# Two token tiles, three weight tiles and the last stage's preparation moved into the stages ahead of them

## Chip, cores and metric

The kernel is one program on one core of a Trainium2 chip. The metric is the device time of one execution in microseconds (us), as the median of several runs. TensorE (PE) multiplies, with its weight load shown apart as PEld; VectorE (DVE), ScalarE (ACT) and GpSimd (POOL) do elementwise work; SyncE (SP) issues the DMA transfers. Each engine executes its own instructions in order, and the engines wait for each other by semaphores.

## The reference, cut to what matters

The reference is a chain of four layers over 2048 tokens of width 512. Each layer adds its result to x. The parts that the change touches are these:

```
# layer 1, second half; layer 2, second half is alike, with a top-2 choice for the gates
base = x @ W_base.T + b_base
h    = einsum('nd,erd->ner', x, A);  moe = einsum('ner,ne,eor->no', h, weights, B) * 2
x    = x_old + base + moe
# layer 2, first half: attention with a paged cache
q, k, v = x @ Wq.T, x @ Wk.T, x @ Wv.T      # then norm, rotation, attention, and o @ Wo.T
# layer 3
y = einsum('bct,bcd->bdt', x, weights[subjects])      # a 32x32 mixing matrix per subject
x = x + y @ W.T + bias + sum over e of (coeffs*scales)[e] * (y @ A[e].T) @ Bf[e].T
```

## The kernel before

All arithmetic is float32, done as three matmuls on a high part and a low part of each operand (`mm3`, line 195). A high part is made by a copy on ACT, and the low part by a subtraction on DVE (`low_part`, line 200) or, for some weight tiles, on POOL. So a tile costs one ACT pass, then one DVE or POOL pass, before PE can use it.

The program is a sequence of stages, and each is a block in which every engine has its own program. At the end of a block all engines meet before any starts the next one. Memory that a stage takes for itself is free only inside it. The stages here are, in order:

- `moe(..., 1, Tables)`, the first mixture. It makes x2. It works on 16 tiles of 128 tokens, and stores each to HBM. Per tile, PE does the gates (12 matmuls of 138 columns into `pl`), one transposition of the weighted low-rank activations (`pt`, line 1628), the base product of the next tile (12 of 512 columns, into `po`) and the three matmuls that add the low-rank part to `po`. DVE computes the gates (lines 1531 to 1583), adds `po` to the old x in `xr` (line 1606, "the add"), makes the low part of `hT` and of a later input tile. `whole(tt + 1)` on PE waits until the add of tile tt-1 is done, since `po` has two banks. POOL adds the bias to each `xr` (line 1479) as soon as its old x has landed.
- `l2_qkv`, the projection. 8 groups of columns by 16 token tiles make 128 steps. Each has 24 matmuls, 12 of 512 and 12 of 256 columns. At its head SP fetches three weight tiles (`w.fetch`, line 134), waits for the last stores of x2, fetches two token tiles, then the fourth weight tile into the slot that the first one leaves. PE transposes two token tiles (line 1942), ACT and DVE split weights and tokens, and PE starts step 0 when all four weight tiles and the first token tile are split.
- `l2_attn`, the attention, and `l2_out`, the output projection. The latter is 4 column blocks by 32 steps of 12 matmuls of 512 columns. POOL has nothing to do in the last half of it.
- `moe(..., 2, Blocks)`, the second mixture. It is as the first, with a top-2 gate. `Blocks` is the work that rides along: it builds the block-diagonal mixing matrices `bd` of layer 3, by 16 masks (line 1378), 4 copies on ACT and 4 low parts on DVE during tiles 2 to 5.
- `l3`, the last stage. It first loads `araw`, `braw` and `whole`, scales `braw`, splits both, multiplies them (24 matmuls into `pm`), adds the product to `whole` and splits that as `base` (called the fold below). Then, per tile, 12 matmuls of 128 columns mix the tokens (`mixed`, into `pc`), ACT and DVE split the result as `cT`, and 12 of 512 columns give `po`. DVE adds it to x, and SP stores.

## Time and profile before

| what | value |
|---|---|
| median of 3 runs | 3490.33 us (3486.12 to 3491.93) |
| the profiled execution, its own time | 3486.69 us |
| its span, first to last instruction | 3484.9 us |
| mean granted clock of TensorE | 0.976 |
| PE busy in the span | 3303.1 us (95%) |
| DVE, ACT, POOL busy | 2325.4, 1764.9, 1369.3 us |

The profiled execution takes 1.8 us more than its span. Since PE is busy nearly everywhere, what matters are the few places where it waits or runs at the lower clock. The two mixtures, the head of the projection and the head of the last stage hold several of them.

### The profile page before, as it was taken

The page shows a single profiled execution, that of the slowest core. Times are in us where ns is not written, and L with a number is a line of the kernel's source. Part 1 is how long each engine was busy: PE and PEld are TensorE (multiplying, and loading weights), DVE is VectorE, ACT ScalarE, POOL GpSimd, SP SyncE. Part 2 cuts the span into 40 slices and gives each one's busy share as a digit, 9 for nine tenths or more (in the row PEclk, how much of TensorE's full clock was granted, in tenths as well). Part 3 has the DMA queues.
Part 4 walks back from the last instruction along what each step waited for, and adds up shares of the span by engine and source line. Part 5 has one row for each costly group of instructions (what it writes and reads, how often), then busy time and mean ns, then how long its engine had stood idle before and what let it go on. Part 6 is the DMA issues. An engine that isn't in the chain of part 4 may idle for free. (4 is left out here: it accounts for less than half of the span.)

```text
span 3484.9 us, 69495 instructions
## 1 busy us (share of the span) xinstructions
PE 3303.1 (95%) x22214; PEld 3048.6 (87%) x22214; DVE 2325.4 (67%) x6609; ACT 1764.9 (51%) x4303; POOL 1369.3 (39%) x2426
## 2 busy tenths in 40 slices
PE   7799799999989999999799999989999998999988
PEld 5688699988878888888799999989999998888877
DVE  6444444445457777778888888888888886322274
ACT  4322222233227778788566666656666665322212
POOL 0221100000017878888556555555555552100022
PEclk9899899999999999999899999999999999999999
DMA  5410532234545555556766666656666666533333
GB/s 204 131 59 26 135 95 81 74 113 130 187 160 162 181 168 179 183 173 206 230 215 218 210 216 216 208 181 207 214 215 213 211 216 195 177 109 109 109 124 124
DMA packets 456501, 571.95 MB, mean 164 GB/s; under 512 B 171657, under 2 KB 341449, under 8 KB 439242
## 3 DMA queue, kind: packets, MB, share of 16 engines
q1 hardware_dynamic: 436426, 429.08, 39.5%
q0 software_dynamic: 19712, 138.42, 11.3%
q8 instruction: 180, 2.95, 0.4%
q14 instruction: 183, 1.50, 0.1%
HBM read 394.60 MB, written 172.75 MB: 163 GB/s over the span
## 5 line engine op out<-in xcount | busy, mean ns | idle before, releaser
L2316 PE MATMUL l2a_x<-l2a_pt,l2a_V 128*128 128x128 f32 x4096 | 542.5, 275 | 4.4 <-DVE l2a_pn L2257 3.6
L2316 PEld LDWEIGHTS l2a_x<-l2a_pt,l2a_V 128*128 128x128 f32 x4096 | 503.2, 193 | 5.0 <-issue 4.9
L2234 DVE CUSTOM_DVE_ANT_0 l2a_sm<-l2a_s,l2a_B 128x544 f32<-128x544 f32 x512 | 369.6, 722 | 92.6 <-PE l2a_s L195 80.4
L1479 POOL TENSOR_TENSOR moe_xr<-moe_xr,moe_bias 128x512 f32<-128x512 f32 x32 | 42.1, 1318 | 960.7 <-DMA moe_xr<-s_x 960.6
L2184 ACT ACTIVATE l2a_p<-l2a_sm,l2a_st 128x544 f32<-128x544 f32 x512 | 379.8, 742 | 27.9 <-DVE l2a_st L2237 27.6
L2043 POOL CAST l2a_K<-cache 128x256 fp32r x768 | 294.4, 433 | 223.4 <-issue 223.4
L2043 POOL CAST keys<-cache 128x256 fp32r x750 | 298.4, 447 | 188.2 <-issue 112.0
L2170 ACT ACTIVATE l2a_pt<-l2a_t 128x512 f32<-128x512 f32 x512 | 305.6, 597 | 128.3 <-PE l2a_t L2302 128.0
L2302 PE MATMUL l2a_t<-ident,l2a_p 128*128 128x128 f32 x2048 | 336.1, 287 | 5.4 <-ACT l2a_ao L2177 5.4
L2302 PEld LDWEIGHTS l2a_t<-ident,l2a_p 128*128 128x128 f32 x2048 | 288.4, 210 | 6.5 <-issue 5.9
L2248 DVE TENSOR_SCALAR l2a_p<-l2a_p,l2a_st 128x512 f32<-128x512 f32 x512 | 280.8, 548 | 18.2
L2177 ACT ACTIVATE l2a_ao<-l2a_x 128x128 f32<-128x128 f32 x512 | 142.0, 277 | 280.8 <-PE l2a_x L2317 280.8
L195 PE MATMUL l2a_s<-keys,head 128*128 128x288 f32 (+1 forms) x1536 | 261.7, 306 | 18.8 <-POOL l2a_K L2043 8.7
L195 PE MATMUL l2q_pa<-keys,cache 128*128 128x512 f32 (+1 forms) x1024 | 268.5, 344 | 0.0
L195 PE MATMUL l2q_pa<-l2q_w1H,cache 128*128 128x512 f32 (+1 forms) x1024 | 267.7, 344 | 0.0
L195 PE MATMUL l2a_s<-l2a_K,l2a_Q 128*128 128x288 f32 (+1 forms) x1536 | 259.9, 305 | 3.4 <-POOL l2a_K L2043 3.0
L1802 POOL TENSOR_TENSOR l2q_rot<-l2q_qs,sinq 128x256 f32<-128x256 f32 x256 | 197.7, 792 | 130.3 <-ACT l2q_qs L1851 130.3
L195 PEld LDWEIGHTS l2a_s<-keys,head 128*128 128x128 f32 x1536 | 214.4, 192 | 19.9 <-issue 13.4
L195 PEld LDWEIGHTS l2a_s<-l2a_K,l2a_Q 128*128 128x128 f32 x1536 | 213.6, 191 | 3.8 <-issue 3.3
L1824 ACT ACTIVATE l2q_qn<-l2q_qn,l2q_r 128x128 f32<-128x128 f32 x640 | 200.3, 397 | 0.8 <-DVE l2q_qn L1917 0.8
L195 PEld LDWEIGHTS l2q_pa<-keys,cache 128*128 128x128 f32 x1024 | 181.0, 190 | 21.7
L195 PEld LDWEIGHTS l2q_pa<-l2q_w1H,cache 128*128 128x128 f32 x1024 | 180.2, 189 | 21.6
(766 smaller groups left out, 8715.1 us busy)
## 6 DMA issues: line engine op xcount, KB each, us to landing
s_qT<-l2q_qo SPq DMA_DIRECT2D x128, 512.0 KB, 2.9
head<-s_qT SPq DMA_DIRECT2D x64, 512.0 KB, 5.8
l2a_Q<-s_qT SPq DMA_DIRECT2D x64, 512.0 KB
s_ao<-l2a_ao SPq DMA_DIRECT2D x64, 512.0 KB, 4.9
l2o_a<-s_ao SPq DMA_DIRECT2D x128, 256.0 KB, 3.0
s_kn<-l2q_ko SPq DMA_DIRECT2D x128, 128.0 KB, 3.1
head<-s_kn SPq DMA_DIRECT2D x32, 512.0 KB, 6.0
l2q_stage<-in_wqkv SPq DMA_DIRECT2D x32, 384.0 KB, 4.1
```

The source lines that it names most:

```text
L195: i = pe.matmul(out, a, b, start=start and m + z == 0, stop=stop and 3 * m + z == n - 1)
L1479: pool.tensor_tensor(xr[tt][:, :], xr[tt][:, :], bias[:, :], ALU.add).then_inc(biased, 1)
L1802: pool.tensor_tensor(r[:, hs, a], q[:, hs, z], sn[:, y, tt, :].unsqueeze(1).broadcast_to([P, hs.stop - hs.start, 64]), ALU.mult).then_inc( ...
L1824: act.activation(o[:, h, :], o[:, h, :], ACT.Copy, scale=f[:, 10 + h:11 + h]).then_inc(scaled, 1)
L2043: e.tensor_copy(K[:, j:j + 1, :, :].rearrange("p a z n -> p a (z n)"), Kall[:, bass.ds(v, 1), :, :].rearrange("p a z n -> p a (z n)")).the ...
L2170: act.activation(ptr[tr % 2][:, :, :], ps_t[tr % 2][:, :, :], ACT.Copy).then_inc(t_copied, 1)
L2177: act.activation(ao[k][:, hg, :, 32 * (g % 2):32 * (g % 2) + 32], ps_x[pv % 2][:, P:256].rearrange("p (h s) -> p h s", h=4), ACT.Copy).the ...
L2184: act.activation(prr[sc % 6][:, :], smr[sc % 2][:, :], ACT.Exp, bias=s[:, 1:2], scale=SCALE, accum_out=s[:, 2:3]).then_inc(exped, 1)
L2234: dve.tensor_tensor_reduce(out=smr[sc % 2][:, :], in0=ps_s[sc % 2][:, 224:768], in1=Br[g % 2][:, :], scale=1.0, scalar=-3e38, op0=ALU.add, ...
L2248: dve.tensor_scalar(p[:, 0:512], p[:, 0:512], s[:, 3:4], None, ALU.mult).then_inc(scaled, 1)
L2302: m = pe.transpose(ps_t[tr % 2][:, k, :], p[:, k:512:4], ident[:, :])
L2316: pe.matmul(px[:, P:256], V[:, k * D + hg * P:k * D + hg * P + P], pt[:, k, :], start=k == 0, stop=False)
```

## The change

In both mixtures the bias is added on DVE (`with_bias`), one tile ahead, and POOL has no work there. Each mixture calls the work that rides along on SP, ACT, DVE and PE.

In the first mixture `Tables` also fetches the first three weight tiles of the projection (tiles 4 to 6) and loads, transposes and splits the first two tiles of x2 (SP in tiles 8 and 9, PE in 11 and 12, ACT in 12 and 13, DVE in 13 and 14). The projection finds them ready. It fetches only the fourth weight tile and begins step 0 with a part for each of the first three weight tiles, as they are split. DVE makes all four low parts there.

`Blocks` moves from the second mixture to the output projection (column block 2). `Fold`, the last stage's preparation, moves into the second mixture. It also loads and splits the first three token tiles of x3. `l3` starts with `mixed(0)`.

The core of the diff:

```diff
     def by_pool(self, k):
-        return self.pooled and k % 3 == 2
+        return self.pooled and k % 3 == 2 and k >= self.own
...
+    def late(self, sp, tt, stores):
+        if 4 <= tt < 7:
+            k = tt - 4
+            sp.dma_start(self.w[k][:, :].unsqueeze(1), rows_of(self.A["wqkv"][0], k, 1)).then_inc(self.w_in[k], 16)
+        if 8 <= tt < 10:
+            t = tt - 8
+            sp.wait_ge(*stores.landed(t, 2))
+            sp.dma_start(self.nat[t][:, :], self.x[t * P:(t + 1) * P, :]).then_inc(self.nat.sem(t), 16)
+
+    def on_vector(self, dve, tt, banks):
+        if 13 <= tt < 15:
+            t = tt - 13
+            dve.wait_ge(self.hi, t + 1)
+            low_part(dve, self.xT[t], banks[t][:, :].rearrange("p (k n) -> p k n", k=4)).then_inc(self.lo, 1)
+
+    def on_scalar(self, act, tt, banks):
+        if 12 <= tt < 14:
+            t = tt - 12
+            act.wait_ge(self.turned, t + 1)
+            act.activation(self.xT[t][0], banks[t][:, :].rearrange("p (k n) -> p k n", k=4), ACT.Copy).then_inc(self.hi, 1)
...
+    def on_tensor(self, pe, tt, banks, weighed):
+
+        if 11 <= tt < 13:
+            t = tt - 11
+            pe.wait_ge(*self.nat.landed(t))
+            pe.wait_ge(weighed, 13 + t)
+            for k in range(4):
+                i = pe.transpose(banks[t][:, k * P:(k + 1) * P], self.nat[t][:, k * P:(k + 1) * P], self.ident[:, :])
+            i.then_inc(self.turned, 1)
...
+    def mask(self, dve, m):
...
+        for j in range(4):
+            dve.tensor_scalar(self.wx(m)[:, :, j, :], self.wg[:, 4 * m:4 * m + 4, :], self.jm[:, j:j + 1], None,
+                              ALU.mult).then_inc(self.masked, 1)
+
+    def high(self, act, m):
+        act.wait_ge(self.masked, 4 * m + 4)
+        act.activation(self.bd[0][:, 4 * m:4 * m + 4, :, :], self.wx(m), ACT.Copy).then_inc(self.hi, 1)
+
+    def low(self, dve, m):
+        dve.wait_ge(self.hi, m + 1)
+        low_part(dve, sl(self.bd, S_, slice(4 * m, 4 * m + 4), S_, S_), self.wx(m)).then_inc(self.lo, 1)
+
+
...
+    def late(self, sp, tt, stores):
+        if tt == 1:
+            sp.dma_start(self.whole[:, :, :], rows_of(self.A["base3"], 0, 4)).then_inc(self.whole_in, 16)
+        if 6 <= tt < 9:
+            t = tt - 6
+            sp.wait_ge(*stores.landed(t, 2))
+            sp.dma_start(self.xn[t][:, :], self.src[t * P:(t + 1) * P, :]).then_inc(self.xn.sem(t), 16)
+
+    def on_scalar(self, act, tt, banks):
+        if tt == 2:
+            act.wait_ge(self.a_in, 16)
+            act.activation(self.a3[0][:, :, :], self.araw[:, :, :], ACT.Copy).then_inc(self.a_hi, 1)
...
+        if tt == 4:
+            act.wait_ge(self.b_scaled, 2)
+            act.activation(self.b3[0][:, :, :], self.braw[:, :, :], ACT.Copy).then_inc(self.b_hi, 1)
+        if 8 <= tt < 11:
+            t = tt - 8
+            act.wait_ge(*self.xn.landed(t, 1))
+            act.activation(self.xh[t][0][:, :], self.xn[t][:, :], ACT.Copy).then_inc(self.x_hi, 1)
+        if tt >= 12:
+            k = tt - 12
+            act.wait_ge(self.folded, k + 1)
+            act.activation(self.base[0][:, k, :], self.whole[:, k, :], ACT.Copy).then_inc(self.base_hi, 1)
+
+    def on_vector(self, dve, tt, banks):
...
+        if tt == 4:
+            dve.wait_ge(self.a_hi, 1)
+            low_part(dve, sl(self.a3, S_, S_, S_), self.araw[:, :, :]).then_inc(self.a_lo, 1)
+        if tt == 6:
+            dve.wait_ge(self.b_hi, 1)
+            low_part(dve, sl(self.b3, S_, S_, S_), self.braw[:, :, :]).then_inc(self.b_lo, 1)
+        if 9 <= tt < 12:
+            t = tt - 9
+            dve.wait_ge(self.x_hi, t + 1)
+            low_part(dve, sl(self.xh[t], S_, S_), self.xn[t][:, :]).then_inc(self.x_lo, 1)
+        if 12 <= tt < 16:
+            k = tt - 12
+            if k == 0:
+                dve.wait_ge(self.whole_in, 16)
+            dve.wait_ge(self.fold_mm, k + 1)
+            dve.tensor_tensor(self.whole[:, k, :], self.whole[:, k, :], banks[k][:, :], ALU.add).then_inc(self.folded, 1)
+        if tt >= 13:
+            k = tt - 13
+            dve.wait_ge(self.base_hi, k + 1)
+            low_part(dve, sl(self.base, S_, k, S_), self.whole[:, k, :]).then_inc(self.base_lo, 1)
+
+    def on_tensor(self, pe, tt, banks, weighed):
+
+        k = tt - 11
+        if 0 <= k < 4:
+            if k == 0:
+                pe.wait_ge(self.a_lo, 1)
+                pe.wait_ge(self.b_lo, 1)
+            pe.wait_ge(weighed, 13 + k)
+            mm3(pe, banks[k][:, :], [(sl(self.a3, S_, m, slice(k * P, (k + 1) * P)), sl(self.b3, S_, m, S_))
+                                     for m in range(2)]).then_inc(self.fold_mm, 1)
...
-        @block.gpsimd
-        def _(pool):
-            pool.wait_ge(bias_in, 16)
-            for tt in range(NT):
-                pool.wait_ge(*xr.landed(tt, 1))
-                pool.tensor_tensor(xr[tt][:, :], xr[tt][:, :], bias[:, :], ALU.add).then_inc(biased, 1)
...
+            def with_bias(tt):
+                if tt < NT:
+                    dve.wait_ge(*xr.landed(tt, 1))
+                    dve.tensor_tensor(xr[tt][:, :], xr[tt][:, :], bias[:, :], ALU.add).then_inc(biased, 1)
...
                 parts(tt + 4)
-                if tt > 1:
-                    next(side, None)
-                    next(side, None)
+                with_bias(tt + 1)
+                beside.on_vector(dve, tt, pl)
...
                 lora(tt + 1)
+                beside.on_tensor(pe, tt, pl, weighed)
...
-    w = Weights(st, 3, 768, [(*sl(wq[hg % 2], S_, slice(k, k + 1), S_), rows_of(A["wqkv"][hg], k, 1)) for hg in range(8) for k in range(4)])
...
+    w = Weights(st, 3, None, [(*sl(wq[hg % 2], S_, slice(k, k + 1), S_), rows_of(A["wqkv"][hg], k, 1)) for hg in range(8) for k in range(4)],
+                own=4, bufs=S["wq_raw"], sems=S["wq_in"])
...
-            for k in range(3):
-                w.fetch(sp, k)
-            sp.dma_start(tab[:, :], A["table"].rearrange("(a n) -> a n", a=1)[:, 0:16]).then_inc(tab_in, 16)
+            w.fetch(sp, 3)
             for k in range(10, 16):
                 sp.wait_ge(*before_x.landed(k))
-            x_tile(0)
-            x_tile(1)
-            w.fetch(sp, 3)
             x_tile(2)
             x_tile(3)
+            sp.dma_start(tab[:, :], A["table"].rearrange("(a n) -> a n", a=1)[:, 0:16]).then_inc(tab_in, 16)
...
             for k in range(4):
-                if not w.by_pool(k):
-                    w.low(dve, k)
-            tokens(0)
-            tokens(1)
+                w.low(dve, k)
...
+            def part(n, ks, cols):
+
+                hg, tt = steps[n]
+                return mm3(pe, pa[n % 2][:, cols], [(sl(xT[tt], S_, k, S_), sl(wq[hg % 2], S_, k, cols)) for k in ks],
+                           start=ks[0] == 0, stop=ks[-1] == 3)
+
+            columns = (slice(0, 512), slice(512, 768))
+            for k in range(3):
+                w.ready(pe, k)
+                for cols in columns:
+                    part(0, (k,), cols)
             for n, (hg, tt) in enumerate(steps):
                 if hg == 0:
                     tokens(tt + 2)
-                    pe.wait_ge(x_lo, tt + 1)
+                    if tt >= 2:
+                        pe.wait_ge(x_lo, tt - 1)
                 if tt == 0:
                     w.ready_to(pe, 4 * hg + 3)
                 if n >= 2:
                     pe.wait_ge(v_copied, n - 1)
-                for cols in (slice(0, 512), slice(512, 768)):
-                    i = mm3(pe, pa[n % 2][:, cols], [(sl(xT[tt], S_, k, S_), sl(wq[hg % 2], S_, k, cols)) for k in range(4)])
+                for cols in columns:
+                    i = part(n, range(4) if n else (3,), cols)
...
     parts = [st.pair(f"as{i}", [P, D]) for i in range(4)]
     acc = [[st.ps(f"acc{j}{i}", [P, D]) for i in range(4)] for j in range(2)]
...
                 if k == 31:
                     for m in range(4):
                         i = 4 * cb + m
                         act.wait_ge(out_mm, n + 1)
...
+                if cb == 2 and k % 4 == 0 and k < 16:
+                    blocks.mask(dve, k // 4)
+                if cb == 2 and k % 4 == 3 and k < 16:
+                    blocks.low(dve, k // 4)
...
-                if tt < NT:
+                if NF <= tt < NT:
...
-            sp.dma_start(cf[:, :], A["coef"]).then_inc(cf_in, 16)
-            sp.dma_start(sc[:, :], A["scal"]).then_inc(sc_in, 16)
-            sp.dma_start(braw[:, :, :], rows_of(A["bt3"], 0, 2)).then_inc(braw_in, 16)
-            sp.dma_start(araw[:, :, :], rows_of(A["a3n"], 0, 2)).then_inc(a3_in, 16)
-            tokens(0)
-            tokens(1)
-            sp.dma_start(whole[:, :, :], rows_of(A["base3"], 0, 4)).then_inc(base_in, 16)
+            tokens(3)
             sp.dma_start(bias[:, :], row_bc(A["b3"], D)).then_inc(bias_in, 16)
-            for tt in range(2, 6):
+            for tt in range(4, 6):
...
-            pe.wait_ge(a_lo, 1)
-            pe.wait_ge(b_lo, 1)
-            for k in range(4):
-                if k >= 2:
-                    pe.wait_ge(folded, k - 1)
-                mm3(pe, pm[k % 2][:, :], [(sl(a3, S_, m, slice(k * P, (k + 1) * P)), sl(b3, S_, m, S_)) for m in range(2)]).then_inc(fold_mm, 1)
-            pe.wait_ge(bd_made, 4)
             mixed(0)
             mixed(1)
...
                     pe.wait_ge(added, tt - 2)
                 pe.wait_ge(c_lo, tt + 1)
-                if tt == 0:
-                    pe.wait_ge(base_lo, 4)
                 mm3(pe, po[tt % 3][:, :], [(sl(cT[tt % 3], S_, k, S_), sl(base, S_, k, S_)) for k in range(4)]).then_inc(out_mm, 1)
                 mixed(tt + 2)
```

Where instructions stand is shown at three places. In such rows and in those of the trace, `moe` names either mixture where buffer numbers are left out. The first is DVE in the first mixture, in the middle of the loop, around the add of tile 3 (`xr3`). Before:

```order
L1583 TENSOR_TENSOR moe1_hw5<-moe1_pl1,moe1_sm1 128x128
L1606 TENSOR_TENSOR moe1_xr3<-moe1_xr3,moe1_po1 128x512
L200 TENSOR_TENSOR moe1_hT0L<-moe1_pt0,moe1_hT0H 128x128
L200 TENSOR_TENSOR cache<-moe1_dr4,cache 128x512
L1531 TENSOR_REDUCE moe1_sm2<-moe1_pl2 128x1
L1533 RECIPROCAL moe1_sm2<-moe1_sm2 128x1
```

After, the same place:

```order
L1708 TENSOR_TENSOR moe1_hw5<-moe1_pl1,moe1_sm1 128x128
L1737 TENSOR_TENSOR moe1_xr3<-moe1_xr3,moe1_po1 128x512
L200 TENSOR_TENSOR moe1_hT0L<-moe1_pt0,moe1_hT0H 128x128
L200 TENSOR_TENSOR cache<-moe1_dr4,cache 128x512
L1719 TENSOR_TENSOR moe1_xr4<-moe1_xr4,moe1_bias 128x512
L1656 TENSOR_REDUCE moe1_sm2<-moe1_pl2 128x1
L1658 RECIPROCAL moe1_sm2<-moe1_sm2 128x1
```

Between the low part of the input tile and the gates of the next tile there is one more pass of 128x512, the bias for tile 4.

The second place is SP from the last stores of the first mixture into the projection (`l2q_stage` and `wqraw` are raw weight tiles, `l2q_nat` raw token tiles). Before:

```order
L1470 DMA s_x<-moe_xr 128x512 x5
L1435 UNCONDITIONAL_BRANCH
L1713 UNCONDITIONAL_BRANCH
L134 DMA l2q_stage<-in_wqkv 128x768 x3
L1747 DMA l2q_tab<-in_table 1x16
L1719 DMA l2q_nat<-s_x 128x512 x2
L134 DMA l2q_stage<-in_wqkv 128x768
L1719 DMA l2q_nat<-s_x 128x512 x3
```

After:

```order
L1601 DMA s_x<-moe_xr 128x512 x5
L1566 UNCONDITIONAL_BRANCH
L1846 UNCONDITIONAL_BRANCH
L134 DMA wqraw<-in_wqkv 128x768
L1852 DMA l2q_nat<-s_x 128x512 x2
L1883 DMA l2q_tab<-in_table 1x16
L1852 DMA l2q_nat<-s_x 128x512
```

Three weight fetches and two token fetches have gone from the head, and the fetch of the fourth weight tile comes first, ahead of the token tiles 2 and 3.

The third place is DVE from the end of the second mixture into the last stage (`moe_` is the mixture, `l_` the last stage). Before:

```order
L1606 TENSOR_TENSOR moe_xr<-moe_xr,moe_po 128x512
L1435 UNCONDITIONAL_BRANCH
L2551 UNCONDITIONAL_BRANCH
L2565 TENSOR_TENSOR l_cw<-l_cf,l_sc 128x2
L2569 TENSOR_SCALAR l_braw<-l_braw,l_cw 128x512 x2
L200 TENSOR_TENSOR l_a3L<-l_araw,l_a3H 128x1024
L200 TENSOR_TENSOR l_b3L<-l_braw,l_b3H 128x1024
L200 TENSOR_TENSOR l_xh0L<-l_xn,l_xh0H 128x512
L200 TENSOR_TENSOR l_xh1L<-l_xn,l_xh1H 128x512
L2579 TENSOR_TENSOR l_whole<-l_whole,l_pm 128x512 x4
L200 TENSOR_TENSOR l_baseL<-l_whole,l_baseH 128x512 x4
```

After:

```order
L200 TENSOR_TENSOR moe_hT3L<-moe_pt,moe_hT3H 128x128
L1719 TENSOR_TENSOR moe_xr<-moe_xr,moe_bias 128x512
L1505 TENSOR_TENSOR moe_whole<-moe_whole,moe_pl 128x512
L200 TENSOR_TENSOR base3L<-moe_whole,base3H 128x512
L1737 TENSOR_TENSOR moe_xr<-moe_xr,moe_po 128x512
L1505 TENSOR_TENSOR moe_whole<-moe_whole,moe_pl 128x512
L200 TENSOR_TENSOR base3L<-moe_whole,base3H 128x512 x2
L1566 UNCONDITIONAL_BRANCH
L2662 UNCONDITIONAL_BRANCH
L200 TENSOR_TENSOR l_cT0L<-l_pc,l_cT0H 128x512
```

The fold's passes now stand in the mixture's last tiles, three of them behind the last add, and the first thing that DVE does in the last stage is the low part of the first mixed tile.

## Rows read from the trace of the kernel before

**Rows 1.** Busy time by stretch: projection, output projection; PE, PEld, DVE, ACT, POOL, clock, DMA

```profile
core 0: us, PE busy (x) PEld busy (x) DVE busy (x) ACT busy (x) POOL busy (x), PEclk, DMA share, GB/s
1126.00:1196.00 70.00, 70.00 (x427) 62.38 (x426) 55.30 (x105) 56.35 (x154) 58.29 (x77) 1.00 0.56 178
3110.00:3200.00 90.00, 90.00 (x398) 74.51 (x398) 22.84 (x33) 23.04 (x38) 0.00 (x0) 1.00 0.35 109
```

**Rows 2.** Timeline, head of the projection: start, duration, engine, instruction, [idle before]

```profile
1028.58 1.31 SPq L134 DMA_DIRECT2D l2q_stage<-in_wqkv  x3
1033.72 0.33 SPq L134 DMA_DIRECT2D l2q_stage<-in_wqkv  x1
1035.16 1.97 PE L1942 MATMUL l2q_pt<-ident,l2q_nat 128*128 128x128 f32 x8 [8.06 <-DMA l2q_nat<-s_x]
1037.22 0.84 ACT L138 ACTIVATE keys<-l2q_stage 128x768 fp32r<-128x768 f32 x1 [1.89 <-DMA l2q_stage<-in_wqkv]
1038.10 0.96 DVE L143 TENSOR_TENSOR head<-l2q_stage,keys 128x768 fp32r<-128x768 f32 x1 [3.44 <-ACT keys L138]
1046.62 0.70 ACT L1851 ACTIVATE l2q_qs<-l2q_pa 128x640 f32<-128x640 f32 x1 [5.09 <-PE l2q_pa L195]
```

**Rows 3.** Waits of PE in the first mixture (936 to 1028): total, times, longest

```profile
PE moe_po L195 <- DVE moe_xr L1606: 2.3, 3, 1.1
PE moe_po L195 <- DVE cache L143: 1.7, 1, 1.7
```

**Rows 4.** The same in the second mixture (3300 to 3396)

```profile
PE moe_po L195 <- DVE moe_xr L1606: 7.9, 6, 2.0
PE moe_po L195 <- DVE moe_hT3L L200: 0.9, 1, 0.9
```

**Rows 5.** Timeline, second mixture: one DVE instruction twice, and POOL beside the second

```profile
3320.93 0.17 DVE L1566 CUSTOM_DVE_ANT_0 moe_sm<-moe_sm 128x8 f32<-128x8 f32 x1
3346.47 1.27 DVE L1566 CUSTOM_DVE_ANT_0 moe_sm<-moe_sm 128x8 f32<-128x8 f32 x1
3346.45 1.28 POOL L1479 TENSOR_TENSOR moe_xr<-moe_xr,moe_bias 128x512 f32<-128x512 f32 x1 [5.08 <-DMA moe_xr<-s_x]
```

**Rows 6.** Timeline of both mixtures: transpositions, the DVE passes behind them, PE behind an add

```profile
986.16 0.29 PE L1628 MATMUL moe_pt<-ident,moe_hw 128*128 128x128 f32 x1
986.80 0.29 DVE L200 TENSOR_TENSOR moe_hT3L<-moe_pt,moe_hT3H 128x128 fp32r<-128x128 f32 x1 [0.88 <-ACT moe_hT3H L1507]
990.13 0.68 DVE L1606 TENSOR_TENSOR moe_xr<-moe_xr,moe_po 128x512 f32<-128x512 f32 x1
991.09 0.29 PE L1628 MATMUL moe_pt<-ident,moe_hw 128*128 128x128 f32 x1
3360.44 0.29 DVE L200 TENSOR_TENSOR moe_hT0L<-moe_pt,moe_hT0H 128x128 fp32r<-128x128 f32 x1 [1.05 <-ACT moe_hT0H L1507]
3363.64 0.69 DVE L1606 TENSOR_TENSOR moe_xr<-moe_xr,moe_po 128x512 f32<-128x512 f32 x1 [0.15 <-PE moe_po L195]
3318.26 0.68 DVE L1606 TENSOR_TENSOR moe_xr<-moe_xr,moe_po 128x512 f32<-128x512 f32 x1
3318.99 0.51 PE L195 MATMUL moe_po<-moe_baseH,ahead 128*128 128x512 f32 x1 [1.66 <-DVE moe_xr L1606]
```

**Rows 7.** Timeline, last stage: four DVE passes of 128x512 with both inputs in SBUF

```profile
3413.98 2.49 DVE L200 TENSOR_TENSOR l_baseL<-l_whole,l_baseH 128x512 fp32r<-128x512 f32 x4
```

**Rows 8.** Chain that ended last, in order of time, head of the last stage

```profile
3396.11 0.33 SPq L2493
...
3397.46 4.99 DMA l_araw<-in_a3n
...
3406.07 7.28 PE l_pm L195 x24
...
3417.72 3.07 PE l_po L195 x12
3420.80 1.29 PE l_pc L195 x12
```

**Rows 9.** Timeline: PE entering the second mixture, and SP's last stores in it

```profile
3300.39 7.92 PE L195 MATMUL moe_pl<-ahead 128*128 128x136 f32 x36 [2.96 <-PEq L2347]
3379.21 16.48 SPq L1470 DMA_DIRECT2D s_x<-moe_xr  x5
```

193 lines of the change are left out of this document (89 added, 104 removed).

## Prediction

> **What bounds the kernel now.** I read the busy time by stretch first. In the long projection PE is busy in all of the 70 us of a stretch, DVE in 55.3, ACT in 56.4 and POOL in 58.3; in the output projection PE is busy in 90 of 90 us, and DVE and ACT in 22.8 and 23.0 [rows 1]. So PE sets the time there, and a gain can only come from where PE waits or runs at half rate. The waits and timelines show four such places: the head of the projection [rows 2], the loops of the two mixtures [rows 3, 4], and the head of the last stage, where the chain that ended last leaves PE for a load, for ACT and for DVE [rows 8]. The change touches exactly these four. I take them in turn, against the profiled execution's own time of 3486.69 us.
>
> **Bias on DVE, both mixtures.** Two things move. First, DVE no longer shares its time with a busy POOL. The same instruction takes 0.17 us alone and 1.27 us where it starts 0.02 us behind a POOL bias of 1.28 us; it ends when POOL does [rows 5]. The Trainium skill (SBUF — State Buffer, "Who interferes with whom") says that a DVE instruction that uses the port shared with GpSimd is held for the whole of the other's instruction, and counts among these any DVE instruction with two SBUF inputs. By that rule 32 holds of up to 1.28 us would vanish, up to 41 us of DVE time; the trace says that only PE's waits for DVE can be won. These are 2.3 and 1.7 us in the first mixture and 7.9 and 0.9 in the second [rows 3, 4].
>
> Second, DVE pays 16 biases in each mixture. Four passes of this size with both inputs in SBUF take 2.49 us, so 0.6 us one [rows 7]. Does it show? Between a transposition and PE's use of the add that depends on it lie: 0.64 us to the next DVE pass, 3.33 us from there to the add, and 0.73 us from the add's start to PE: 4.70 us in the first mixture. In the second the middle piece is 3.20 less the 0.15 that DVE waited, so 3.05, and the chain is 4.42 [rows 6]. PE itself goes from one transposition to the next in 4.93 us [rows 6], so both chains are hidden. With 0.6 more they are 5.30 and 5.02: late by 0.37 and 0.09. A late PE makes its next transposition late too, so every second round has slack, and half of it counts: 0.18 and 0.05 us a round. Over 12 rounds that is 2.2 us and 0.5 us. What could be dearer: at POOL's price, 1.28 us a bias [rows 5], 0.34 us more a round, 4 us more in each mixture. At nothing, the 2.7 us are gained instead. I take 0.6, since rows 7 are of the same engine, size and memory.
>
> **First mixture.** Of its waits of 2.3 us the last, about 0.7 us, ends with PE's own last matmuls and stays, so 1.6 and 1.7 go. The bias costs 2.2. Eight transpositions are added; 12 matmuls of 128 columns take 1.29 us [rows 8], so these take 0.9, of which 0.4 fall into the lateness above. ACT and DVE passes for the two token tiles come when DVE has no more input tiles to split. The five loads on SP have many rounds ahead of them. Sum: 3.3 - 2.2 - 0.5 = 0.6 us gained.
>
> **Head of the projection.** Before, from SP's first issue (1028.58) to ACT's first copy of a result (1046.62) pass 18.0 us [rows 2]. After, call the stage's start B. ACT splits the first weight tile at once (0.84), DVE makes its low part (0.96 [rows 2]), so at B+2.0 both SP may fetch the fourth tile and PE may start. The fetch took 3.5 us before (1033.72 to 1037.22), then 0.84 and 0.96 follow [rows 2]: B+7.4. PE meanwhile does 18 matmuls at half rate. In the last stage 24 matmuls of 512 columns that began cold took 7.28 us, and 12 warm ones take 2.86 [rows 8]; 7.28 - 5.72 = 1.6 us is what a cold start costs once. Warm, a quarter of a step (3 of 512, 3 of 256 columns) is 1.1 us. Three of them and the loss are 4.9, so PE is at B+6.9, transposes a token tile (0.5), and finishes the last quarter at B+8.5. Gain: 18.0 - 8.5 = 9.5 us. It hangs on the fourth tile: the loads that SP issued at 1028.58 in a bunch made ACT wait longer, and with 2 us more for this load the gain is 7.5. If PE stays at half rate throughout, 1 us goes.
>
> **Masks in the output projection.** Four times DVE gets about 0.9 us of masks and, three steps on, 0.7 us of low part; a step there is 2.7 us, of which DVE uses a quarter [rows 1]. PE hides it. Without that cover it would be 6 us. Cost: 0.
>
> **Second mixture.** All waits for adds but none of the work go: 7.9 + 0.9 = 8.8 us, the last 1.5 of them filled by folding matmuls. Added are 24 folding matmuls, 5.7 at the warm pace [rows 8]; the bias, 0.5; two low parts of 128x1024 on DVE (tiles 4 and 6), twice the size of rows 7, 1.2 us each against a chain without slack, so 2.3; and three low parts of x3 tiles, 0.6 each at half weight, 0.9. SP's new loads are issued behind those that the loop needs. Sum: 8.8 - 5.7 - 0.5 - 2.3 - 0.9 = -0.6.
>
> **Head of the last stage.** Before, SP ends its last store issue at 3379.21 + 16.48 = 3395.69 [rows 9], the stage begins at 3396.11, and PE's first real output matmul starts at 3417.72 [rows 8]: 22.0 us. After: behind the last add stand an addition to `whole` and two low parts, the second behind an ACT pass, 2.0 us; the last add itself comes 0.5 later, since DVE is still busy with a piece of the fold. SP issues its last store (0.33, as an issue in [rows 8]) beside this, and entering the stage takes 0.42 (3395.69 to 3396.11). So PE begins to mix 2.0 + 0.5 - 0.33 + 0.42, about 2.5 us, after the point from which the 22.0 were counted. PE has then idled 3 us, as it had at 3300.39, where 36 short matmuls took 7.92 us, 0.22 each, against 0.11 warm [rows 8, 9]. So 24 mixing matmuls take 5.3 us, which covers ACT and DVE on the first mixed tile, and the first output block loses 1.6 us to the clock as `pm` did. That is 2.5 + 5.3 + 1.6 = 9.4 against 22.0: 12.6 us gained. Warm from the start it would be 3 us less, bounded by ACT and DVE on the first tile; with 3 us more at half rate, 1.5 more.
>
> **Sum.** 0.6 + 9.5 + 0 - 0.6 + 12.6 = 22.1 us. The profiled execution would take 3464.6 us; the median of the runs, 3490.33, lies 3.6 above the profiled one, so it becomes 3468.2. I say 3468.
>
> **Rivals.**
> - *The clock rises within the mixing* (the last stage gains 3 us more), or the chains in the mixtures have more slack than I give them (2.7 more): about 3463. For it: `pm` was warm after some 3 us. Against: 36 short matmuls stayed at half rate [rows 9]. 0.2.
> - *DVE becomes the bound of both mixtures.* A round then loses 0.5 us and not 0.18, because a pass waits for its old x or costs more than 0.6; 8 to 10 us go back: 3477. DVE is the engine that PE waits for already [rows 4]. 0.1.
> - *The change doesn't do what it says at the projection*: the fourth weight tile and the stores of x2 set its start as before, 5 us of 9.5 are not won: 3473. For it: the fetch still stands behind DVE's first low part. Against: it has no token tiles ahead of it. 0.1.
> - *Slower.* The projection is 128 steps in a fixed rhythm, where POOL has only 12 of 70 us idle [rows 1]. If the new phase between DVE and POOL at its head makes them hold each other [rows 5] so that PE waits in each step, it costs 128 times the wait. From 0.17 us a step on it eats the whole gain; at 0.25 us the time is 3500. Against: 70 of 70 us busy, over many phases of the weight work. 0.03.
>
> **How the numbers follow.** The forecast itself has 0.55, the rivals 0.2, 0.1, 0.1, 0.03, and 0.02 is for anything else. The median of before spans 5.8 us over three runs, and 0.2% is 7 us, about what a measurement can tell. The forecast's own range is 3465 to 3472. To leave out no more than 2 in 10, 3459 to 3477 takes in the first three rivals and the bounds of bias and load. Faster 0.95, within 0.2% 0.02, slower 0.03.
>
> **What would show it.** Right: no waits of PE for `xr` over 0.6 us in the mixtures, but many small ones; ACT's first copy in the projection some 8.5 us after SP's first issue; `l_pc` matmuls 0.22 us apart at the head of the last stage and the first `l_po` 8 us behind the last store issue; no new wait in the output projection. Wrong: waits on `moe_xr` loads by DVE, a fourth weight tile that lands later than 5.5 us into the projection, or PE waits between its steps.

## The result

The changed kernel takes **3457.87 us** (median of 4 runs, 3452.21 to 3460.31) against 3490.82 for the kernel before on the same chip (4 runs, 3486.12 to 3491.93). The ratio is 0.9906, 95% interval [0.9889, 0.9923], so 27 to 39 us of gain. I forecast 3468 and 22 us, with 3459 as the lower end: the sign and the places were right, the size was 11 us short, and the measured time lies 1.1 us under the range. The profiled execution took 3457.95 us, its span is 3456.2.

The page of the changed kernel gives span and busy time:

```profile
span 3456.2 us, 69511 instructions
PE 3306.9 (96%) x22214; PEld 3052.9 (88%) x22214; DVE 2328.6 (67%) x6640; ACT 1766.3 (51%) x4305; POOL 1325.0 (38%) x2393
```

Busy time by stretch, the same two as in [rows 1] (the columns are those named there):

```profile
1126.00:1196.00 70.00, 70.00 (x428) 62.38 (x427) 55.42 (x105) 56.28 (x153) 58.42 (x77) 1.00 0.53 169
3110.00:3200.00 90.00, 90.00 (x398) 74.52 (x398) 27.61 (x52) 26.75 (x45) 0.00 (x0) 1.00 0.35 110
```

PE is still busy in all of both. The masks are now visible in the second, as 4.8 us more of DVE and 3.7 of ACT than in [rows 1], and PE does not feel them.

Timeline of the changed kernel at the head of the projection, beside [rows 2]:

```profile
1023.07 2.31 ACT L138 ACTIVATE keys<-wqraw 128x768 fp32r<-128x768 f32 x3 [3.07 <-PEq L1566]
...
1024.93 0.33 SPq L134 DMA_DIRECT2D wqraw<-in_wqkv  x1
1024.96 0.80 PE L195 MATMUL l2q_pa<-keys,cache 128*128 128x512 f32 x1 [3.44 <-DVE head L143]
...
1028.13 0.84 ACT L138 ACTIVATE keys<-wqraw 128x768 fp32r<-128x768 f32 x1 [2.75 <-DMA wqraw<-in_wqkv]
...
1029.01 0.96 DVE L143 TENSOR_TENSOR head<-wqraw,keys 128x768 fp32r<-128x768 f32 x1 [2.37 <-ACT keys L138]
...
1032.25 0.71 ACT L1977 ACTIVATE l2q_qs<-l2q_pa 128x640 f32<-128x640 f32 x1 [0.44 <-PE l2q_pa L195]
```

From ACT's first pass to its first copy of a result pass 9.2 us; I had said 8.5. The fourth weight tile landed after 3.2 us and not 3.5.

Waits of PE in the changed kernel, for the first mixture (to 1023) and then the second, beside [rows 3, 4]:

```profile
PE moe_po L195 <- DVE moe_hT3L L200: 0.9, 1, 0.9
PE moe_po L195 <- DVE moe_xr L1737: 0.7, 1, 0.7
...
PE moe_pl L195 <- PEq L2481: 3.0, 1, 3.0
PE moe_po L195 <- DVE moe_xr L1737: 2.1, 3, 0.9
PE moe_po L195 <- DVE moe_btL L143: 0.4, 1, 0.4
```

What is left for `moe_xr` in the second mixture are 2.1 us, where there were 7.9.

The chain that ended last, head of the last stage, beside [rows 8]:

```profile
3382.14 5.35 PE l_pc L195 x24
3387.49 5.04 PE l_po L195 x12
3392.53 1.29 PE l_pc L195 x12
3393.82 2.83 PE l_po L195 x12
```

It now begins with PE itself. The 24 mixing matmuls run at half rate as forecast (5.35 us, granted clock 0.50), and so does nearly the whole first `l_po`: 5.04 against 2.83 in the next, 2.2 us lost where I had 1.6.

### Where the gain sits

I cut each profile at the same events: PE's first gate matmul of a mixture, PE's last matmul in it, ACT's first copy in the projection. Before was profiled five times in all and the changed kernel three times (the added ones are experiments below). Means and ranges, in us:

| stretch | before | changed | gain | forecast |
|---|---|---|---|---|
| start to first mixture (code unchanged) | 935.8 (932.4 to 937.4) | 933.3 (932.5 to 934.2) | 2.5 | 0 |
| first mixture | 91.1 (89.7 to 92.7) | 88.4 (88.2 to 88.6) | 2.7 | 0.6 |
| its end to ACT's first copy in the projection | 19.5 (18.5 to 19.9) | 10.6 (10.5 to 10.7) | 8.9 | 9.5 |
| from there to the second mixture | 2255.1 (2253.8 to 2257.1) | 2254.3 (2252.1 to 2255.4) | 0.9 | 0 |
| second mixture | 94.9 (92.5 to 96.1) | 91.7 (91.2 to 92.2) | 3.2 | -0.6 |
| its end to the end of the kernel | 91.9 (90.3 to 93.5) | 76.8 (75.9 to 77.5) | 15.1 | 12.6 |
| sum | 3488.3 | 3455.0 | 33.3 | 22.1 |

The trace on which the forecast was built has 937.4, 89.7, 19.5, 2253.8, 94.2 and 90.3 in these rows. The first mixture and the last stage stand there at or next to the lower end of what the kernel before does, and the code ahead of the first mixture next to the upper end.

### The profile page after: what moved, and what is told of

It is laid out like the page before. It is cut to its first block and busy times, and to the rows that moved or that the text cites. A ratio compares the mean times of both kernels' runs of the same rounds, so it can differ in the third digit from the quotient of the medians.

```text
span 3456.2 us, 69511 instructions
## 1 busy us (share of the span) xinstructions
PE 3306.9 (96%) x22214; PEld 3052.9 (88%) x22214; DVE 2328.6 (67%) x6640; ACT 1766.3 (51%) x4305; POOL 1325.0 (38%) x2393
## 5 line engine op out<-in xcount | busy, mean ns | idle before, releaser
L2367 DVE CUSTOM_DVE_ANT_0 l2a_sm<-l2a_s,l2a_B 128x544 f32<-128x544 f32 x512 | 369.9, 722 | 94.2 <-PE l2a_s L195 81.8
L195 PEld LDWEIGHTS l2a_s<-keys,head 128*128 128x128 f32 x1536 | 214.7, 192 | 18.5 <-issue 11.8
```

The costliest lines, as they stand in the source:

```text
L195: i = pe.matmul(out, a, b, start=start and m + z == 0, stop=stop and 3 * m + z == n - 1)
L2367: dve.tensor_tensor_reduce(out=smr[sc % 2][:, :], in0=ps_s[sc % 2][:, 224:768], in1=Br[g % 2][:, :], scale=1.0, scalar=-3e38, op0=ALU.add, ...
```

## The experiments

The surplus is the 11 us by which the gain is larger than forecast. Theory at first: the terms of the forecast are right within their bounds, and the surplus is chance or one mis-sized term. Rivals: it belongs to one part that does more than I said, or the parts do not add. A hold, below, is a DVE instruction that takes longer because a POOL instruction runs beside it.

### Parts undone, one at a time

**The bias alone.** Everything but the bias as before:

```diff
-            for tt in range(NT):          # POOL
-                pool.tensor_tensor(xr[tt][:, :], xr[tt][:, :], bias[:, :], ALU.add).then_inc(biased, 1)
+                with_bias(tt + 1)         # DVE, behind parts(tt + 4)
```

> Of the change only the bias on DVE, in both mixtures; projection, masks and last stage as before. Terms on record: first mixture 3.3 - 2.2 = 1.1 us gained, second 8.8 - 0.5 = 8.3 us, together 9.4: about 3481.4 from a median of 3490.8. PE waits for DVE of about 1 us in the middle of a round of the first mixture, none over 0.6 in the second. Rival 'DVE gets full': the biases cost what the holds did, 3488 to 3491. Rival 'the surplus sits here': the part of the 33 us that no term explains (about 8 to 10) comes from the bias, 3472 or less.

Measured: 3483.64 against 3488.42, ratio 0.9987 [0.9979, 0.9996]: 1 to 7 us gained. That is less than 9.4. The first mixture took 88.0, the second 93.1: 3.1 and 1.8 us under the means of before, where the terms had 1.1 and 8.3. Of the waits for adds in the second mixture that [rows 4] show as 7.9 us, this is left, without POOL:

```profile
PE moe_po L195 <- DVE moe_xr L1631: 4.5, 3, 1.9
```

So most of them were not POOL's doing.

**The bias on POOL, all else changed** (the reverse edit in the changed kernel).

> The changed kernel with the bias back on POOL, all else as changed. If the terms add, 9.4 us are given back: about 3467 from 3457.9. If DVE is so full of the fold's passes that its holds by POOL cost more now, 3470 or more. If the bias gave nothing once the second mixture carries the fold, 3458 to 3460.

Measured: 3465.52, ratio 0.9930 [0.9917, 0.9942]. Against the changed kernel's 0.9906 to 0.9912 that gives 6 to 8 us back. First mixture 92.9, second 97.7: 4.5 and 6.0 over the changed kernel, more than the bias won alone (3.1 and 1.8). By one profile of each the parts do not add. The medians do not settle it, since 6 to 8 us back and 1 to 7 us won overlap, and 7.6 lies near the 9.4 of the terms. With DVE's bias the side work is nearly free in the first mixture (88.0 without it, 88.4 with it).

**The projection's part undone**: loads, transpositions and the order of the projection's head as before.

> The changed kernel with the projection and the first mixture's side work as before (no early fetch, no early transposes; bias on DVE stays). Terms on record: head 9.5, side work -0.5: 9 us given back, 3467. The trace of the changed kernel shows 8.8 us at the head. Rival 'the surplus sits in the projection's new start': over 12 us given back, 3470 or more, with the difference between the head and the second mixture.

Measured: 3470.67, ratio 0.9949 [0.9936, 0.9963]. The head took 20.5 where the changed kernel has 10.5 to 10.7 and the kernel before 18.5 to 19.9. The profiled span stands 10.4 to 16.5 us above those of the changed kernel, the median 13 us above its median. That median is what the rival asked for (3470 or more). In the profile only 9.9 of the 12.9 us over the mean of the changed kernel are at the head, and the other 3 are spread over all other stretches but the first mixture. So the head gives 9 to 10 us, and a surplus there is not shown.

**The last stage's part undone**: masks beside the second mixture, fold in the last stage.

> The changed kernel with masks in the second mixture and the last stage's preparation in the last stage, as before; bias on DVE stays. Terms on record: 12.6 us given back at the head of the last stage, 8.9 us of side work taken off the second mixture: 3457.9 + 3.7 = 3461.6. Rival 'the fold is hidden in the second mixture' (its 24 matmuls fill waits that stay without them): up to 12.6 given back, 3470. Rival 'fold costs more than thought' : 3458 or less.

Measured: 3474.86, ratio 0.9963 [0.9950, 0.9976], 17 us over the changed kernel where I expected 3.7. End of the second mixture to the end of the kernel: 90.7, 14 us more. But the second mixture, rid of the fold, was not 9 us shorter; it took 93.2, longer than with the fold, because the masks were back in it. The expectation had left them out.

**Nothing beside the second mixture**: masks in the output projection, fold in the last stage.

```diff
-            st = moe(nc, A, S, st, 2, Fold)
+            st = moe(nc, A, S, st, 2, Nothing)   # and l3 does the fold itself, as before
```

> The changed kernel with nothing beside the second mixture: masks stay in the output projection, but the last stage's preparation is done in the last stage as before. Head of the last stage 23 us again, +14.5. Terms on record: the second mixture loses 8.9 us of fold, so 3459 + 12.6 - 8.9 = 3463. Rival 'the 24 matmuls are all that the fold costs' (two 128x1024 low parts and three x3 low parts hidden): second mixture 91.2 - 5.7 = 85.5, 3468. Rival 'the fold fills waits': second mixture 88 or more, 3471 or more.

Measured: 3467.34, ratio 0.9932 [0.9918, 0.9945]; second mixture 86.7. These are the waits of PE in the second mixture, first with masks only (the run before), then with nothing:

```profile
PE moe_po L195 <- DVE moe_xr L1656: 6.1, 5, 1.9
...
PE moe_po L195 <- DVE moe_hT3L L200: 0.9, 1, 0.9
```

```profile
PE moe_po L195 <- DVE moe_hT3L L200: 0.9, 1, 0.9
PE moe_po L195 <- DVE moe_xr L1664: 0.7, 1, 0.7
```

So the masks cost 6.5 us there even without POOL: in four rounds DVE gets two more pieces, 0.9 and 0.7 us. The fold costs 5.0: 6.6 in the rounds and behind them, less 1.7 at the entry, where the changed kernel came from its first gate to the second transposition in 15.7 to 16.6 us and this run in 17.8. I had booked the fold's 24 matmuls, its two long low parts and its x3 tiles as 8.9 of new cost.

The second mixture in steps, as means where there are several profiles: 94.9 before, 93.1 to 93.5 with the bias on DVE (three profiles), 86.7 with the masks gone too, 91.7 with the fold in it. My forecast took all of PE's waits for adds there as POOL's doing; the masks had most of them.

### What makes the kernel before scatter

**Changed kernel and kernel before, profiled again.**

> The changed kernel as it is, profiled again. The four changed places should repeat within 1 us: first mixture 88.4, head of the projection 10.7, second mixture 91.2, head of the last stage 8.6. If the 4.3 us by which the unchanged work ahead of the first mixture was shorter is chance, that piece comes out anywhere from 932 to 937 and the median lies at 3488.4 - 26 to 28 = 3460 to 3462. Rival 'it is an effect of the change': 933.1 again and a median of 3456 to 3458.

> The kernel before, profiled again. Two things are open: whether the 937.4 us ahead of the first mixture (931.9 to 935.5 in eight profiles of kernels with the same code there) were chance, and where the 3.6 to 5.5 us sit by which the medians of before lie above its profiled execution. If chance: 932 to 936 ahead of the first mixture, and the mixtures, heads and the rest longer than 89.7, 19.5, 94.2, 23.1 by some us. If it is an effect of how the kernel before lies in memory: 937 again, and the same in every stage.

> The kernel before a third time, one look: the same question as for its second profile.

> The changed kernel a third time. Mixtures 88.5 and 91.4 within 0.3 again, since no engine shares DVE's time; the stages ahead of the first mixture anywhere in 931 to 937 if their scatter is chance.

Measured: changed 3460.57 and 3457.25, ratios 0.9912 [0.9897, 0.9928] and 0.9909 [0.9894, 0.9924]; before against itself 1.0006 [0.9996, 1.0016], with the second profile at 3493.47 and the third at 3494.63 us. The waits in the second profile of before, first and second mixture:

```profile
PE moe_po L195 <- DVE moe_xr L1606: 4.2, 5, 1.2
...
PE moe_po L195 <- DVE cache L143: 1.3, 1, 1.3
...
PE moe_po L195 <- DVE moe_xr L1606: 5.5, 4, 2.0
```

In the third:

```profile
PE moe_po L195 <- DVE moe_xr L1606: 4.7, 7, 1.2
...
PE moe_po L195 <- DVE moe_xr L1606: 8.7, 6, 2.6
```

No two are alike, nor like [rows 3, 4]. The time from one transposition of PE to the next (a round; start to start, worked out from the timelines) shows it, for the first mixture, second to eighth interval:

| kernel | rounds, us |
|---|---|
| before, first profile | 5.02, 4.87, 5.69, 4.88, 4.87, 4.88, 4.93 |
| before, second | 6.05, 4.87, 5.48, 6.31, 4.88, 4.88, 4.92 |
| before, third | 6.10, 4.87, 5.46, 6.30, 4.88, 5.90, 4.92 |
| before, fourth | 5.86, 4.86, 4.87, 5.87, 4.88, 4.88, 4.92 |
| before, fifth | 4.93, 4.87, 5.84, 4.87, 4.88, 5.07, 4.92 |
| changed, first | 4.93, 5.23, 4.93, 5.21, 4.95, 5.21, 4.99 |
| changed, second | 4.92, 5.23, 4.90, 5.26, 4.89, 5.27, 4.93 |
| changed, third | 4.92, 5.23, 4.90, 5.25, 4.91, 5.24, 4.96 |

The changed kernel repeats itself within 0.07 us here. In the second mixture its first round varies (5.6, 5.9 and 6.5) and the others repeat as well. When POOL starts, a load decides: of 615.5 us of POOL's idle time before its 16 additions, 615.4 end with the landing of an old x (second profile, first mixture). The timeline of the same profile shows POOL and DVE meeting in the second mixture:

```profile
3331.32 0.87 DVE L1378 TENSOR_SCALAR moe_wx<-wg,moe_jm 128x128 f32<-128x128 f32 x4
...
3332.89 0.69 DVE L200 TENSOR_TENSOR bdL<-moe_wx,bdH 128x512 fp32r<-128x512 f32 x1 [0.70 <-ACT bdH L1389]
...
3333.59 1.28 POOL L1479 TENSOR_TENSOR moe_xr<-moe_xr,moe_bias 128x512 f32<-128x512 f32 x1 [3.69 <-DMA moe_xr<-s_x]
...
3334.04 0.86 DVE L1556 CAST moe_sm<-moe_ix 128x2 f32<-128x2 uint32 x1
...
3337.07 0.50 PE L195 MATMUL moe_po<-moe_baseH,moe_dT5H 128*128 128x512 f32 x1 [2.04 <-DVE moe_xr L1606]
...
3340.44 0.17 DVE L1556 CAST moe_sm<-moe_ix 128x2 f32<-128x2 uint32 x1
```

The same cast of 128x2 elements takes 0.17 us alone and 0.86 beside POOL, and ends 0.03 us after POOL does. It is in a chain of small steps that ends in `moe_xr`. The wait of 2.04 us is not all its work, for the same round carries a mask step and its low part (0.87 and 0.69).

Over whole mixtures the two causes part. I compared each DVE instruction of a mixture with the shortest of its kind there (same line, tiles and shape). In each of the 15 mixtures in which POOL works (two in each of seven profiles, one in the kernel that moves only the second bias), 7 to 12 DVE instructions take over 0.12 us longer, in sum 4.8 to 9.8 us, and every one of them overlaps a POOL instruction. In the 25 mixtures without POOL not a single one does. So POOL lengthens DVE's work in every execution, at other places each time.

**Is it the hold, or the wait for POOL's result?** One run without any bias, and one in which POOL works at the same points on data that nobody uses:

```diff
+                pool.tensor_tensor(junk[:, :], bias[:, :], bias[:, :], ALU.add).then_inc(biased, 1)
...
-                dve.wait_ge(biased, tt + 1)
+                dve.wait_ge(*xr.landed(tt, 1))
```

> Leaves out the addition of the bias in both mixtures (32 DVE instructions of the changed kernel), all else as changed. By the terms on record the biases cost 2.2 us in the first mixture and 0.5 in the second once POOL no longer holds DVE: 2.7 us faster, first mixture 86.2, second 90.7. Rival 'hidden': both as they were. Rival 'DVE is the bound': 0.68 us a round for 12 rounds in each, 12 us or more faster in all.

> As the run without a bias, but POOL does an addition of the same size at the same points on tiles that nobody else reads or writes (bias + bias into a spare tile), so nobody waits for POOL. The output lacks the bias. If POOL's work holds DVE's (the theory on record): mixtures near those with the bias on POOL, 92.9 and 97.7 less at most 1 us each, and 10 us over the run without bias: 3463. Rival 'the gain came from no longer waiting for POOL's result': 87 and 90 as without a bias, 3453.

Measured: without bias 3453.34, ratio 0.9892 [0.9877, 0.9907]; with POOL beside it 3458.44, ratio 0.9911 [0.9894, 0.9927]. First to last transposition: 72.5 and 77.2 us in the two mixtures without, 75.2 and 80.2 with POOL. POOL's instructions were shorter here, 1.04 against 1.28 us. So its mere presence costs 2.6 and 3.0 us in this pair of profiles, nobody waiting for it (1.8 and 4.6 over the whole mixtures): the hold is real, though smaller than the 10 us expected. With POOL doing the true bias the two stretches were 79.0 and 84.9. That is no proof of a wait for POOL's result, for there the holds were longer too: 8.3 and 8.8 us in sum against 5.3 and 4.8. The two are not parted. The Trainium skill (SBUF — State Buffer, "Who interferes with whom") names the cast among the instructions that can take the ports shared by DVE and GpSimd, when their operands meet certain conditions, and says that the first to issue keeps them for its whole instruction; the 0.86 us cast agrees.

The run without bias also prices DVE's: 74.5 - 72.5 = 2.0 us in the first mixture (2.2 forecast) and 2.0 in the second (0.5 forecast). In the second it falls where DVE has side work: the rounds with the fold's long low parts take 5.46 and 5.45 us without the bias and 6.03 and 6.05 with it, the one with the last x3 tile 4.89 and 5.49.

**Two more looks at before, and a kernel between.**

> Before, one look. Chance: 931 to 936 ahead of the first mixture. Effect of the change: 936 to 938. Mixtures 89.5 to 93 and 94 to 97 in either case, scattered.

> Before, one more look, with the same expectation: 931 to 936 ahead of the first mixture if the difference is chance, 936 to 938 if it is an effect; mixtures scattered.

> Of the change only the bias of the second mixture on DVE; POOL keeps the bias of the first. If POOL's work is what makes a mixture scatter: second mixture as with the bias alone (93.1 to 93.2, the same round times within 0.1), first between 89.7 and 92.5 with late rounds at other places than in any run before. Time between before and the bias alone: 3486 to 3489.

Measured: 3490.65 and 3488.32 us; ahead of the first mixture 935.8 and **932.4**. The last value lies within those of the runs made from the changed kernel, with the same code there (930.6 to 935.5), so the 2.5 us in the unchanged code are no effect that these runs can establish. The kernel with only the second bias moved: 3487.43, ratio 0.9992 [0.9983, 1.0001]; first mixture 92.4 with rounds of 8.97, 6.16 and 6.45, second 93.5. Its four long rounds, 7.07, 6.33, 6.32 and 6.37, are those of the run with only the last stage undone (7.08, 6.28, 6.33, 6.37). The run with the bias alone had the same mixture code and two rounds of 8.6 instead, so without POOL there are two patterns, not one.

### Single prices in the changed kernel

**The two low parts of 128x1024, halved:**

```diff
-        if tt == 4:
-            low_part(dve, sl(self.a3, S_, S_, S_), self.araw[:, :, :]).then_inc(self.a_lo, 1)
+        if 4 <= tt < 6:
+            low_part(dve, sl(self.a3, S_, tt - 4, S_), self.araw[:, tt - 4, :]).then_inc(self.a_lo, 1)
...                                                    # b3 likewise in tiles 6 and 7
```

> The changed kernel with the two low parts of 128x1024 (the fold's a3 and b3) cut into four of 128x512, one in each of tiles 4 to 7. If each long pass makes one round late by 1.1 us (6.02 and 6.05 against 4.9): two such rounds go, four of 5.2 to 5.5 come, 1 us gained in the second mixture, the rest as in the changed kernel. If lateness is not linear but a matter of slack: nothing is late but by 0.2, 2 us gained. Rival: the wait moves to the fold matmuls, no change.

Measured: 3458.65, ratio 0.9916 [0.9902, 0.9929], no difference in the median. In the profile the rounds of 6.02 and 6.05 became 5.49 and 5.50, with no other round longer by more than 0.2: 1 us, as the first theory said, and too little for the run times to tell.

**Matmuls that nobody reads, where PE only waits for a stage to end:**

```diff
+            idle_matmuls(pe, pt[0][:, :], hT[3][0][:, :], bt[0][:, 0, :], 6 if kind == 1 else 12)  # end of moe
+            idle_matmuls(pe, pa[1][:, 0:512], xT[0][0][:, 0, :], xT[0][0][:, :, :], 7)             # head of l2_qkv
+            idle_matmuls(pe, acc[0][0][:, :], wo[0][:, 31, 0:P], parts[3][0][:, :], 11)            # end of l2_out
```

> The changed kernel with matmuls whose result nobody reads, put where PE has nothing to do but wait for a stage to end: 11 behind the output projection, 6 behind the first mixture and 7 at the head of the projection, 12 behind the second mixture, each 512 columns. If idle time is what takes the clock down: first gates of the second mixture 36 in 4 us and not 5.8 to 7.9 (2 to 4 gained), 24 l_pc in 2.7 and not 5.2 and the first l_po 12 in 2.8 and not 5.0 (4.7 gained), 1 to 2 us in the projection's head: 7 to 9 us under the changed kernel, 3450. Rival: the clock falls anyway over the stage's boundary, or matmuls of zero use hold the stage's end: no change or up to 2 us slower.

> The run with unread matmuls at stage ends, and 15 more of them around the last block of the stage ahead of the first mixture (7 while PE waits for DVE's td, 8 behind its last matmul). There 24 matmuls of 256 columns ran 0.21 us apart against 0.12, and the 36 first gates took 4.7 to 6.9 against 4.2 warm: 2 us and 1 to 2 us to be gained. 3449 against 3452.6. Rival: what follows waits for DVE and the weights anyway, 3452 or more.

> Halved low parts, and unread matmuls behind the first mixture (6), at the head of the projection (7) and behind the second mixture (12), none behind the output projection. The head of the projection 1 us and the last stage 4.5 to 5 us shorter, second mixture 1 to 2: 6 to 8 us under the changed kernel. If the matmuls behind the output projection were of use, it is slower than the run that had them.

Measured: 3452.64, 3456.89 and 3451.72, ratios 0.9893 [0.9878, 0.9908], 0.9898 [0.9882, 0.9915] and 0.9894 [0.9881, 0.9908]; the changed kernel beside them 0.9912, none on that chip, and 0.9909. The first has all the lines above. The second has 15 more unread matmuls ahead of the first mixture and was no faster for them, as its rival had it (3452 or more). The third has the halved low parts and leaves out those behind the output projection. The profiles split it by place. Chain of the first of the three, head of the last stage:

```profile
3380.93 1.54 PE l_pc L195 x12
...
3382.49 0.60 ACT l_cT0H L2664
```

Twelve mixing matmuls in 1.54 us, not at half rate, and now the chain goes over ACT, because PE is no longer the slower. From the end of the second mixture's own matmuls to the end of the kernel pass 73.0 us in all three, against 75.9 to 77.5 in the changed kernel and 75.5 to 77.4 in other runs with its last stage, so 2.5 to 4.5 us are won. At the projection's head no gain is shown: 9.9, 10.2 and 9.9 us, and 9.9 to 10.7 in runs without unread matmuls. At the head of the second mixture nothing is won:

```profile
3285.22 4.21 PE L195 MATMUL moe_pl<-ahead 128*128 128x136 f32 x36 [0.47 <-PEq L2489]
3290.56 0.79 PE L195 MATMUL moe_po<-moe_baseH,ahead 128*128 128x512 f32 x1 [1.13 <-DVE moe_baseL L143]
```

That is the first of these kernels. The gates took 4.21 us (granted clock 1.00) instead of 7.92 in the third, which has no unread matmuls there, and PE then waited for the weights' low parts, with the clock down again (0.50 from 3290.60 to 3293.00). From the first gate to the second transposition it took 16.7 us with them and 16.6 without. At the head of the first mixture, in the second of the kernels, the same:

```profile
936.49 4.21 PE L195 MATMUL moe_pl<-keys 128*128 128x138 f32 x36 [0.50 <-PEq L1010]
943.45 2.08 PE L195 MATMUL moe_po<-cache,keys 128*128 128x512 f32 x4 [2.75 <-DVE cache L143]
```

The third kernel is the fastest of the study by median, 5 to 6 us under the changed one, but its interval overlaps with that of the changed kernel (0.9881 to 0.9908 and 0.9894 to 0.9924 on one chip).

## Why the prediction missed

**What bounds the kernel, and where the gain comes from**: right. The four places that the forecast named hold 29.9 of the 33.3 us, and the output projection hid the masks.

**Bias on DVE, first mixture**: right in mechanism and in price. The forecast's alternation, every second round with slack, is what the trace shows (4.93, 5.21), and its cost came out at 2.0 for 2.2. What was short is what it saves: the bias alone brought the mixture to 88.0 us, 1.7 under the one trace and 3.1 under the mean of five, where 1.1 was forecast.

**The steps that failed.** Forecast and result, 3468.2 and 3457.9, are 10.3 us apart. Two steps make up 7.2 of them, and 2.9 are open.

- *The term for the second mixture*, -0.6 us: measured 3.0 in the pair of first profiles, 3.6 too low. "24 folding matmuls, 5.7 at the warm pace" cost 3.4, the x3 tiles 0.5 for 0.9, and some 1 us came at the mixture's entry. The fold as a whole cost 6.6 and not 8.9 (next paragraph).
- *The base*: "the median of the runs, 3490.33, lies 3.6 above the profiled one, so it becomes 3468.2". That took the 3.6 us for something that stays. For the changed kernel the profiled execution and the median are alike (3457.95 and 3457.87). The five profiles of before have 91.1 and 94.9 in the mixtures where the one read has 89.7 and 94.2, and 91.9 behind the second where it has 90.3, in sum 3.8 us, and -0.3 in the rest. So the 3.6 may well have been in the places that the change cleans up, but five profiles do not prove it, and one execution's own scatter is as large: the standard deviation is 3.3 us over 69 executions of before and 3.5 over 12 of the changed kernel. The mixtures became regular, the whole time did not.
- The other 2.9 us are unchanged stretches of the first pair of profiles.

PE's waits themselves were not read too low throughout. For the adds of the first mixture they are 2.3 us in the one trace and 3.1 to 4.7 in the other four, for those of the second 7.9 and 5.4 to 8.7.

**Second mixture**: -0.6 forecast, 3.2 measured (3.0 in the pair of first profiles). The step without the fold was nearly right in size: 8.3 us for the waits less the bias, and from the second transposition to the last the kernel before took 75.5 us against 66.8 with nothing beside. But that is luck in part, for the bias cost 2.0 and not 0.5, the waits gone were mostly those of the masks and not of POOL's bias, and 1.6 us of waits remain. Some 1 us of the pair's gain stands at the entry (16.7 us from the first gate to the second transposition against 15.7), where the level of PE's clock differs from one profile to the next; I count it as chance. The rest, 2.3 us, is the fold. The two long low parts were right: rounds of 6.02 and 6.05 against 4.9, 2.3 us, as forecast. The x3 tiles cost 0.5 and not 0.9 (a round of 5.50 against 4.96). The 24 matmuls cost 3.4 us and not 5.7 (6.26, 4.95 and 4.94 against 4.86, 3.61 and 4.50 in the last rounds, and 0.3 behind them): PE had 1.6 us of waits at that place without them, and none in the changed kernel. I had seen that ("the last 1.5 of them filled by folding matmuls") and then booked all 24 at full price.

**Head of the projection**: 9.5 forecast, 8.9 measured. The fetch took 3.2 us for 3.5, and PE's first three quarters of a step 5.6 for 4.9; no term is wrong by more than 0.7.

**Last stage**: 12.6 forecast, 12.8 in the pair of first profiles, 15.1 over all. In my trace the first `l_po` took 3.07 us [rows 8]; the chain of the second profile of before has it at half rate:

```profile
3408.64 7.77 PE l_pm L195 x24
...
3420.79 5.49 PE l_po L195 x12
...
3427.80 2.86 PE l_po L195 x12
```

Three of the five profiles of before pay such a price there, which I had booked as new for the changed kernel. The changed kernel loses 1.8 to 2.3 us to it, not 1.6.

**The sum.** 33.3 = 22.1 + 3.8 (terms wrong in the first pair: 0.7, 3.6, -0.7 and 0.2) + 2.9 (unchanged stretches of that pair) + 4.6 (that pair against the mean of all profiles), within rounding.

**The rivals.** "The clock rises within the mixing, or the chains have more slack" was nearest in size but not in cause: in two of three profiles the clock did not rise within the mixing (5.35 and 5.36 us, 0.22 each), in the third it did (3.76 us), and the rounds had no more slack. DVE did not become the bound of both mixtures: the bias cost 2.0 us in each, against 8 to 10 in both by that rival. The projection gained what it should, and its rhythm did not suffer: 70 of 70 us busy.

**What stays open.** The 2.5 and 0.9 us in stretches with unchanged code. One of five profiles of before is as short ahead of the first mixture as the changed kernel, so chance is likely and not proven. So is the share of the 3.6 us that was chance. It is also not shown why the masks, without POOL, fall into one of two patterns of late rounds.

## What to carry to other kernels

Where two engines hold each other and a load decides when they meet, one trace shows one outcome of many: take a second and third profile before summing its waits, and ask whether the distance between the profiled run and the median will stay. A wait names the engine waited for and not what filled it: with POOL's bias gone, 4.5 us (6.1 in the run with only the last stage undone) of 7.9 us of waits in the second mixture were still there, and went with the masks. Moving the bias off POOL alone made the first mixture regular and won 3.1 us there where its waits had promised 1.1. Side work is nearly free in a round that has slack and costs its price in one that has none. Unread matmuls in PE's idle time at a stage's end paid where PE itself came next on the path, and paid nothing where the next thing was a wait for a weight.

## What was unexpected in the hardware

- A DVE cast of 128x2 elements took 0.86 us instead of 0.17 beside a POOL addition, and POOL's mere presence cost 2.6 and 3.0 us a mixture, one profile against one, with nobody waiting for it. No DVE instruction of a mixture was longer than its shortest like by over 0.12 us unless POOL was working beside it.
- The same POOL addition took 1.28 us with two distinct inputs, written onto one of them, and 1.04 (24 of 32) with the same tile for both and another for the result.
- PE's clock level at a stage's entry differs between executions of one kernel. In the kernel before the first `l_po` took 3.07 us in two profiles (granted clock 1.00), 4.34 in one (0.67) and 5.49 in two (0.50), each time with the same wait of 1.8 us ahead of it. Twelve unread matmuls of 512 columns in the idle time ahead of the last stage took its 24 mixing matmuls from 5.35 to 2.87 us.
